# Causal attention on Trainium2: one GpSimd instruction for the P remainders of two key tiles, and another order of the row tiles for the maxima

## The chip, the cores and the metric

The kernel runs on one core of one Trainium2 chip, in one launch. The metric is device time in microseconds (us) from the start of the program to its end, as the median of several runs. Lower is better.

## What is computed

A post-norm decoder layer on x of shape (4, 1024, 512): self attention with 16 heads of 32 columns, then attention over a context with a mask, then a quantised gated feed-forward network, each with a residual sum and a layer norm. The change touches only the self attention, of which the reference says:

```python
bias = alibi_bidirectional_bias(H, S, x.dtype)
scores = jnp.einsum('bhqd,bhkd->bhqk', q, k) * (1.0 / np.sqrt(hd)) + bias[None]
attn = jax.nn.softmax(scores, axis=-1)
out = jnp.einsum('bhqk,bhkd->bhqd', attn, v)
```

The bias is causal in half of the heads (a query sees the keys up to itself) and anti-causal in the other half (a query sees the keys from itself on), with -1e9 elsewhere. So of the 8 x 8 blocks of 128 queries by 128 keys of a head only 36 are worked on.

## The kernel before

The phases run one after the other: preparation, self attention, output projection, cross attention, feed-forward. Self attention and cross attention share one function, `attention_phase`, with `causal` true or false.

There are 4 x 16 = 64 heads, taken one after the other, even ones causal and odd ones anti-causal. A head goes through two streams of 8 units each, with unit number u = 8 x head + k:

- **Maxima.** TensorE computes the scores of one row tile of 128 queries against the keys that it sees (L871, 1 to 8 blocks wide) into one of two PSUM tiles `sc`. VectorE adds the ALiBi strip and takes the row maximum (L1076). It then counts up `taken`, and TensorE may write that PSUM tile again. `rows_of` gives the order of the row tiles. When the 8 maxima of a head are there, TensorE turns them into a row (L879), ScalarE copies it (`mrow`, L987) and a DMA puts it under the queries as one more contraction row.
- **Keys.** TensorE computes the transposed scores of one key tile, less the maximum, in chunks of up to 512 queries into one of two PSUM tiles `st` (`key_scores`, L905 and the diagonal mask L908). ScalarE takes the exponential into `p32` (L979, one instruction a chunk). The upper 16 bits of each fp32 number are P's high part. GpSimd subtracts them from the number and writes the remainder to `plo` as fp16 (`low`, L1164). TensorE multiplies both parts by the values (`values`, L934 and L935) into `ob`, which holds the head's output over its 8 key tiles. `keys_of` gives the order: widths 8, 1, 7, 2, 6, 3, 5, 4 blocks. That order isn't changed.

At the end of a head ScalarE copies the high half of the output (`oraw`, L1029), VectorE adds the low half (`osum`, L1099), and with these reads TensorE may start the values of the next head. Later VectorE takes the reciprocal of the denominators (L1105) and scales the output, reading `osum` and `rden` from SBUF and writing `ost` (L1112). This last instruction stands behind the maximum of the step t with t % 8 = 2 (`SCALE`).

Each engine has one in-order queue, written out step by step. In step t TensorE issues the row scores of unit t + 19 (`SLEAD`), the key scores of unit t + 6 (`ELEAD`) and the values of unit t. VectorE does the maximum of unit t + 19, ScalarE the exponentials of unit t + 6, GpSimd the remainder of unit t + 5. For the 8 steps of a head the widths in blocks are, before the change:

```
step t % 8            0  1  2  3  4  5  6  7
row scores, maxima    2  6  3  5  4  8  1  7
key scores, exp       5  4  8  1  7  2  6  3
values                8  1  7  2  6  3  5  4
```

Below, R8 is the row scores of 8 blocks, M8 their maximum, K4 and E4 the key scores and exponentials of the key tile of 4 blocks, V8 the values of the tile of 8. `p32` and `plo` are rings of NPP buffers, each with two units in it (`spot`). Exponentials of unit u wait until the values of unit u - PAIR x NPP are done. Two lines set who waits for whom at the row scores and at the values:

```python
pe.wait_ge(taken, i * (HB * UH) + slot + 1)
pe.wait_ge(o_read, (i * HB + n) * 2 + 2)
```

The first, with `taken` started at 2, holds the row scores of a unit until the maximum of the unit two before is done. The second holds V8, the first values of a head, until both `osum` additions of the head before are done.

Of the kernel before, what the change touches and what calls it, by code (L numbers as in the profile page):

```python
# [27 lines left out]
P = 128  # L28
B, S, D = 4, 1024, 512
# [20 lines left out]
class Kit:  # L50
# [11 lines left out]
    def sb(self, name, shape, dt):  # L62
        return self.ctx.enter_context(self.nc.sbuf_tensor(name, shape, dt))
# [473 lines left out]
UH = ST  # L537
INPUT = tuple(range(ST))
BIG_FIRST = (7, 0, 6, 1, 5, 2, 4, 3), (0, 7, 1, 6, 2, 5, 3, 4)
SCALE = 2  # L540
HB = 4
NI = B * H // HB
# [2 lines left out]
PAIR = 2  # L545


def attention_phase(nc, c, name, causal, q_dram, k_dram, v_dram, out_dram, mb_dram=None, nm_dram=None, place_dram=None, kept=None, spare=None):
# [12 lines left out]

    with ExitStack() as ctx:
        kit = Kit(nc, ctx)
        SLEAD, ELEAD, NPP = 19, 6, 4
        NPR = PAIR * NPP
        PW = PAIR * S
        sem = lambda n: kit.sem(f"{name}_{n}")
        sb = lambda n, s, d: kit.sb(f"{name}_{n}", s, d)
        qa = [sb(f"qa{j}", [P, S], F16) for j in range(NQK)]
# [2 lines left out]
        vh = [sb(f"vh{j}", [P, ST, VW], F16) for j in range(NQK)]  # L572
        p32 = [sb(f"p32_{j}", [P, PW], F32) for j in range(NPP)]
        plo = [sb(f"plo{j}", [P, PW], F16) for j in range(NPP)]
        junk = [sb(f"junk{j}", [P, S], BF16) for j in range(2)]
# [49 lines left out]
        def query_range(n, kt):  # L625
            if not causal:
                return 0, S
            return (kt * P, S) if n % 2 == 0 else (0, (kt + 1) * P)

        def rows_of(u):  # L630

            n, k = divmod(u, UH)
            return n, k, (BIG_FIRST[n % 2] if causal else INPUT)[k]

        def keys_of(u):

            n, k = divmod(u, UH)
            return n, k, (BIG_FIRST[1 - n % 2] if causal else INPUT)[k]

# [33 lines left out]
        def to_finish(i, t, late):  # L673

            n, k = divmod(t, UH)
            return n - 1 if k == late and (n > 0 or not isinstance(i, int) or i > 0) else None

        def on_vector(u):

            return not causal and u % UH == 4  # L680

        def width(u):

            n, k, kt = keys_of(u)
            a, z = query_range(n, kt)
            return z - a

        def spot(u):

            return u // PAIR % NPP, 0 if u % PAIR == 0 else S  # L690

        def high_of(u):

            j, b = spot(u)
            return p32[j][:, b:b + width(u)].bitcast(BF16).rearrange("p (q h) -> p q h", h=2)[:, :, 1]

        def lows_of(u):

            j, b = spot(u)
            if on_vector(u) or not causal and u % PAIR == 0 and not on_vector(u + 1):  # L700
                return None
            if not causal and u % PAIR == 1 and not on_vector(u - 1):
                return j, 0, b + width(u)
            return j, b, b + width(u)

        def lows_by(u, vector):

            if vector:
                return sum(on_vector(m) for m in range(u + 1))
            return sum(lows_of(m) is not None for m in range(u + 1)) + (lows_of(u) is None)  # L710

        LV, LG = lows_by(HB * UH - 1, True), sum(lows_of(m) is not None for m in range(HB * UH))

        def within(last, u):
# [3 lines left out]
        with nc.Block() as block:  # L718

            @block.sync  # L720
            def _(sp):
# [28 lines left out]
                def store(i):  # L750

                    sp.wait_ge(o_scaled, i * HB + HB + 1)
                    columns = ds(i % (H // HB) * (HB * HD), HB * HD)
                    if causal:
                        out = out_dram[ds(i // (H // HB) * S, S), columns].rearrange("(t p) n -> p t n", p=P)
                    else:
                        out = kept[:, ds(i // (H // HB) * ST, ST), columns]
                    sp.dma_start(out, ost[:]).then_inc(o_out, 16)
# [7 lines left out]
                def step(i, t, last, next_batch=None, first=False):  # L766
                    n, k = divmod(t, UH)
                    if t == SCALE + 2 and not first:
                        store(i - 1)
# [85 lines left out]
            def _(pe):  # L855
                def scores(i, u):

                    n, at, qt = rows_of(u)
                    j, slot = n % NQK, u
                    if at == 0:  # L860
                        pe.wait_ge(qk_in[j], (i + n // NQK + 1) * QKS)
                    pe.wait_ge(taken, i * (HB * UH) + slot + 1)
                    if not causal:
                        nc.tensor.matmul(sc[slot % 2][:, 0:GT], qa[j][0:HD, qt * P:(qt + 1) * P], ka[j][0:HD, 0:GT], start=True, stop=True)  # L864
                        nc.tensor.matmul(sc[slot % 2][:, GT:S], qa[j][HD:2 * HD, qt * P:(qt + 1) * P], kx[j][HD:2 * HD, :],  # L865
                                         start=True, stop=True).then_inc(scored, 1)
                        return
                    k0, k1 = key_range(n, qt)
                    for k in range(k0, k1, GT):
                        w = min(GT, k1 - k)  # L870
                        mm = nc.tensor.matmul(sc[slot % 2][:, k - k0:k - k0 + w], qa[j][0:3 * HD, qt * P:(qt + 1) * P],  # L871
                                              ka[j][0:3 * HD, k:k + w], start=True, stop=True)
                    mm.then_inc(scored, 1)
# [165 lines left out]
            def _(dve):  # L1039
# [43 lines left out]
                def low(i, u):  # L1083
                    n, at, kt = keys_of(u)
                    if not on_vector(u):
                        return
                    dve.wait_ge(expd, i * CS + chunks_by(u) + 2)
                    j, b = spot(u)
                    q = slice(b, b + width(u))
                    nc.vector.tensor_tensor(plo[j][:, q], p32[j][:, q], high_of(u), ALU.subtract).then_inc(lo_v, 1)  # L1090
# [28 lines left out]
                def step(i, t, last):  # L1119
# [4 lines left out]
                    if within(last, t + ELEAD - 3):  # L1124
                        low(i, t + ELEAD - 3)
                    n = to_finish(i, t, SCALE if causal else 0)
                    if n is not None:
# [8 lines left out]
            def _(pool):  # L1136
# [21 lines left out]
                def low(i, u):  # L1158
                    if lows_of(u) is None:
                        return  # L1160
                    pool.wait_ge(expd, i * CS + chunks_by(u) + 2)
                    j, a, z = lows_of(u)
                    high = p32[j][:, a:z].bitcast(BF16).rearrange("p (q h) -> p q h", h=2)[:, :, 1]
                    nc.gpsimd.tensor_tensor(plo[j][:, a:z], p32[j][:, a:z], high, ALU.subtract).then_inc(lo_g, 1)  # L1164
# [942 lines left out]
def decoder_layer(nc, x, context, mask, Wq, bq, Wk, bk, Wv, bv, Wf, bf, w_gate, w_up, w_down, out):  # L2107
    x = x.rearrange("b s d -> (b s) d")
    context = context.rearrange("b s d -> (b s) d")
    mask = mask.rearrange("b o q k -> (b o q) k")  # L2110
    out = out.rearrange("b s d -> (b s) d")

    def scratch(name, shape, dt):
        return nc.dram_tensor(name, shape, dt).ap()

    qk_dram = [scratch(f"scr_{n}", [B, D, S], F16) for n in ("q_hi", "q_lo", "k_hi", "k_lo")]
    q2_dram = [scratch(f"scr_q2_{n}", [B, D, S], F16) for n in ("hi", "lo")]
    k2_dram = [scratch(f"scr_k2_{n}", [B, D, S], F16) for n in ("hi", "lo")]
    v_dram, v2_dram = scratch("scr_v", [B * H, P, ST, VW], F16), scratch("scr_v2", [B * H, P, ST, VW], F16)
    mb_dram, nm_dram = scratch("scr_mb", [T, S], BF16), scratch("scr_nm", [B, S, S], F16)  # L2120
    w_dram = [scratch(f"scr_w_{n}", [3 * FT, P, KT * P], F16) for n in ("hi", "lo")]
    place_dram = scratch("scr_place", [H, S], F16)
    attn, x1_dram = (scratch(n, [T, D], F32) for n in ("scr_attn", "scr_x1"))

    with ExitStack() as ctx:
        c = make_identities(nc, Kit(nc, ctx))
        preparation_phase(nc, c, x, Wq, bq, Wk, bk, Wv, bv, qk_dram, v_dram, context, k2_dram, v2_dram,
                          mask, mb_dram, nm_dram, (w_gate, w_up, w_down), w_dram)
        attention_phase(nc, c, "self", True, qk_dram[0:2], qk_dram[2:4], v_dram, attn, place_dram=place_dram)
        projection_phase(nc, c, attn, x, Wf, bf, x1_dram, q2_dram)  # L2130
        rows = Kit(nc, ctx).sb("rows", [P, RES * T], F32)
        attention_phase(nc, c, "cross", False, q2_dram, k2_dram, v2_dram, None, mb_dram, nm_dram,
                        kept=rows[:, 0:T // P * D].rearrange("p (t n) -> p t n", n=D), spare=rows[:, T // P * D:])
        feed_forward(nc, c, rows, x1_dram, w_dram, scratch, out)
# [21 lines left out]
```

## Time and profile before

| what | value |
|---|---|
| median of 3 runs | 3118.3 us (3116.58 to 3133.7) |
| the profiled execution, its own time | 3118.51 us |
| its span, first to last instruction | 3116.7 us |
| granted TensorE clock, mean | 0.935 |
| self attention, first exponential to last value matmul | 414.4 to 994.4 us |

The profiled execution lies 0.2 us above the median. Its span leaves out 1.8 us around the program. The self attention is 580 us of it, 19%. A row of the profile names line, engine, operation, output and input, and gives busy time and idle time. An engine's instructions in a row can overlap by some 40 ns in these records, since the next is fetched while one ends.

### The profile page before, as it was taken

The numbers are of one execution on the slowest core, as the hardware profiler recorded it, in microseconds if no ns is written. First come the engines' busy times: TensorE is split into PE (matmuls) and PEld (weight loads), VectorE is DVE, ScalarE is ACT, GpSimd is POOL, SyncE is SP. The second block draws the span as 40 slices with busy tenths as digits, with TensorE's granted clock in tenths as the row PEclk, the third lists the DMA queues.
The fourth block names the chain that finished last, engine by engine and source line by source line (L and its number), as shares of the span: only waits on it lengthen the run. The fifth ranks groups of instructions, "written<-read, shape, count | busy, mean of one in ns | idle before, by whom it ended". The sixth has DMA issues, their size and how long they took to land. (4 is left out here: it accounts for less than half of the span.)

```text
span 3116.7 us, 77411 instructions
## 1 busy us (share of the span) xinstructions
PE 2617.6 (84%) x24119; PEld 1411.1 (45%) x24119; DVE 2262.3 (73%) x4461; ACT 1865.0 (60%) x3767; POOL 1817.6 (58%) x1232
## 2 busy tenths in 40 slices
PE   7999578888886868999999999980999899703999
PEld 3555235555554434555555555540444344301444
DVE  8888667777775767788888888857433467697776
ACT  3444257777775435777777777764233577696333
POOL 3444479999997316999999999986100244300000
PEclk9999779999998988999999999995999999856999
DMA  8999824444445652122122232125544588797332
GB/s 303 337 335 339 271 97 135 132 128 134 128 137 163 242 199 69 53 82 69 52 85 61 56 97 55 44 59 183 206 162 161 194 271 288 252 415 279 112 124 81
DMA packets 324185, 513.52 MB, mean 165 GB/s; under 512 B 36757, under 2 KB 158485, under 8 KB 324074
## 3 DMA queue, kind: packets, MB, share of 16 engines
q1 hardware_dynamic: 320938, 505.88, 48.6%
q0 software_dynamic: 1952, 6.29, 0.6%
q8 instruction: 52, 0.85, 0.1%
q14 instruction: 59, 0.48, 0.0%
q10 hardware_dynamic: 1184, 0.01, 0.0%
HBM read 273.18 MB, written 194.28 MB: 150 GB/s over the span
## 5 line engine op out<-in xcount | busy, mean ns | idle before, releaser
L1164 POOL TENSOR_TENSOR cross_plo<-cross_p 128x2048 f16<-128x2048 f32 (+1 forms) x256 | 850.5, 3352 | 120.2 <-ACT cross_p L979 120.2
L1076 DVE CUSTOM_DVE_ANT_0 cross_junk<-cross_sc,rows 128x1024 bf16<-128x1024 f32 x512 | 622.7, 1223 | 159.2 <-PE cross_sc L865 149.7
L979 ACT ACTIVATE cross_p<-cross_st 128x512 f32<-128x512 f32 x1024 | 556.2, 595 | 205.4 <-PE cross_st L910 205.4
L1164 POOL TENSOR_TENSOR self_plo<-self_p 128x1024 f16<-128x1024 f32 (+7 forms) x512 | 577.3, 1166 | 18.7 <-ACT self_p L979 18.6
L979 ACT ACTIVATE self_p<-self_st,self_strip 128x512 f32<-128x512 f32 (+3 forms) x768 | 415.2, 582 | 148.0 <-PE self_st L908 117.2
L1076 DVE CUSTOM_DVE_ANT_0 self_junk<-self_sc,self_strip 128x1024 bf16<-128x1024 f32 (+7 forms) x512 | 371.1, 752 | 140.3 <-PE self_sc L871 135.3
L905 PE MATMUL cross_st<-cross_qa,cross_ka 97*128 97x512 f16 x1024 | 395.4, 386 | 2.4 <-ACT cross_p L979 1.9
L910 PE MATMUL cross_st<-rows,idbig 128*128 128x512 f16 x1024 | 391.0, 382 | 0.0
L934 PEld LDWEIGHTS cross_o<-cross_vh,cross_p 128*128 128x128 bf16 x4096 | 270.0, 97 | 76.3 <-issue 21.9
L934 PE MATMUL cross_o<-cross_vh,cross_p 128*128 128x65 f16 x4096 | 297.4, 191 | 5.1 <-POOL cross_plo L1164 4.7
L1774 POOL TENSOR_SCALAR v_w<-v_w 128x512 f32<-128x512 f32 x96 | 60.1, 626 | 401.5 <-ACT v_w L1751 401.4
L935 PE MATMUL cross_o<-cross_vh,cross_plo 128*128 128x33 f16 x4096 | 291.0, 179 | 0.0
L905 PE MATMUL self_st<-self_qa,self_ka 98*128 98x512 f16 (+3 forms) x768 | 243.8, 333 | 48.6 <-ACT self_p L979 44.1
L935 PEld LDWEIGHTS cross_o<-cross_vh,cross_plo 128*128 128x128 f16 x4096 | 249.2, 96 | 53.4
L871 PE MATMUL self_sc<-self_ka,self_qa 96*128 96x512 f16 (+3 forms) x768 | 212.4, 334 | 58.0 <-DVE self_strips L1050 32.0
L934 PE MATMUL self_o<-self_vh,self_p 128*128 128x65 f16 x2304 | 199.2, 192 | 39.8 <-DVE self_osum L1099 21.0
L130 PE MATMUL gt_acc<-rows,wg_hi 128*128 128x512 f16 x768 | 229.8, 381 | 1.5 <-DVE rows L124 1.5
L864 PE MATMUL cross_sc<-cross_ka,cross_qa 32*128 32x512 f16 x512 | 200.7, 393 | 28.9 <-DMA cross_kx<-scr_k_hi 18.5
L865 PE MATMUL cross_sc<-cross_kx,cross_qa 32*128 32x512 f16 x512 | 200.6, 393 | 0.0
L934 PEld LDWEIGHTS self_o<-self_vh,self_p 128*128 128x128 bf16 x2304 | 163.1, 97 | 74.1 <-issue 43.8
L935 PE MATMUL self_o<-self_vh,self_plo 128*128 128x33 f16 x2304 | 191.9, 179 | 0.0
L905 PEld LDWEIGHTS cross_st<-cross_qa,cross_ka 97*128 97x128 f16 x1024 | 99.7, 97 | 190.1 <-ACT cross_p L979 95.4
(256 smaller groups left out, 5843.8 us busy)
## 6 DMA issues: line engine op xcount, KB each, us to landing
self_strip<-self_strips SPq DMA_DIRECT2D x68, 516.0 KB, 3.2
scr_gate<-gt_y SPq DMA_DIRECT2D x96, 256.0 KB, 2.1
v_w<-scr_gate SPq DMA_DIRECT2D x96, 256.0 KB, 4.1
scr_h<-v_w SPq DMA_DIRECT2D x96, 256.0 KB, 4.2
j_h<-scr_h SPq DMA_DIRECT2D x48, 512.0 KB, 9.5
d_o<-scr_o SPq DMA_DIRECT2D x9, 1536.0 KB
scr_up<-v_y SPq DMA_DIRECT2D x48, 256.0 KB, 4.3
j_u<-scr_up SPq DMA_DIRECT2D x24, 512.0 KB, 12.1
```

The source lines that it names most:

```text
L130: mm = nc.tensor.matmul(out, a, b, start=(n == 0), stop=(n == len(terms) - 1))
L864: nc.tensor.matmul(sc[slot % 2][:, 0:GT], qa[j][0:HD, qt * P:(qt + 1) * P], ka[j][0:HD, 0:GT], start=True, stop=True)
L865: nc.tensor.matmul(sc[slot % 2][:, GT:S], qa[j][HD:2 * HD, qt * P:(qt + 1) * P], kx[j][HD:2 * HD, :], start=True, stop=True).then_inc(scor ...
L871: mm = nc.tensor.matmul(sc[slot % 2][:, k - k0:k - k0 + w], qa[j][0:3 * HD, qt * P:(qt + 1) * P], ka[j][0:3 * HD, k:k + w], start=True, st ...
L905: mm = nc.tensor.matmul(out[:, 0:w], lhs, qa[j][0:KR, q0:q1], start=True, stop=causal)
L910: mm = nc.tensor.matmul(out[:, 0:w], c["idbig"][:], nm[kt][:, q0:q1], start=False, stop=True)
L934: nc.tensor.matmul(out[:, qt % 4, :], high[:, q], vh[n % NQK][:, kt, :], start=first, stop=False, skip_group_check=True)
L935: mm = nc.tensor.matmul(out[:, qt % 4, 0:HD + 1], rest[:, q], vh[n % NQK][:, kt, 0:HD + 1], start=False, stop=last_kt, skip_group_check=True)
L979: nc.scalar.activation(p32[j][:, b + q0 - a:b + q1 - a], stp[cc % 2][:, 0:q1 - q0], ACT.Exp, bias=bias, scale=SM).then_inc(expd, 1)
L1076: nc.vector.tensor_tensor_reduce(junk[slot % 2][:, 0:w], sc[slot % 2][:, 0:w], bias, 1.0, -3e38, ALU.add, ALU.max, qmax[n % 2][:, qt:qt + ...
L1164: nc.gpsimd.tensor_tensor(plo[j][:, a:z], p32[j][:, a:z], high, ALU.subtract).then_inc(lo_g, 1)
L1774: nc.gpsimd.tensor_scalar(wk[n % NW][:], wk[n % NW][:], 65536.0, MAGIC, ALU.mult, ALU.add).then_inc(inc, 1)
```

## The change

In the causal phase the ring gets 8 buffers in place of 4, each 1152 columns wide (9 blocks) in place of 2048. The second unit of a pair stands right behind the first. GpSimd no longer runs a remainder for each unit: at the even unit it does nothing, and at the odd one it does both in one instruction over 1152 columns, since each pair of key tiles has 9 blocks (8 + 1, 7 + 2, 6 + 3, 5 + 4). The values of an even unit therefore wait for the remainder of the pair. The cross attention did this already, and nothing changes there. The row tiles for the maxima come in another order, with widths 8, 7, 1, 2, 6, 5, 3, 4.

```diff
 BIG_FIRST = (7, 0, 6, 1, 5, 2, 4, 3), (0, 7, 1, 6, 2, 5, 3, 4)
+BIG_TWICE = (7, 6, 0, 1, 5, 4, 2, 3), (0, 1, 7, 6, 2, 3, 5, 4)
...
-        SLEAD, ELEAD, NPP = 19, 6, 4
+        SLEAD, ELEAD, NPP = (19, 6, 8) if causal else (19, 6, 4)
         NPR = PAIR * NPP
-        PW = PAIR * S
+        PW = S + P if causal else PAIR * S
...
-            return n, k, (BIG_FIRST[n % 2] if causal else INPUT)[k]
+            return n, k, (BIG_TWICE[n % 2] if causal else INPUT)[k]
...
-            return u // PAIR % NPP, 0 if u % PAIR == 0 else S
+            return u // PAIR % NPP, 0 if u % PAIR == 0 else (width(u - 1) if causal else S)
...
-            if on_vector(u) or not causal and u % PAIR == 0 and not on_vector(u + 1):
+            if on_vector(u) or u % PAIR == 0 and not on_vector(u + 1):
                 return None
-            if not causal and u % PAIR == 1 and not on_vector(u - 1):
+            if u % PAIR == 1 and not on_vector(u - 1):
                 return j, 0, b + width(u)
```

The widths by step are, after it:

```
step t % 8            0  1  2  3  4  5  6  7
row scores, maxima    2  6  5  3  4  8  7  1
key scores, exp       5  4  8  1  7  2  6  3
values                8  1  7  2  6  3  5  4
```

GpSimd's queue in the first four heads, one head of it, before (`self_plo` is the remainder, `self_p32` the numbers; the number behind the name is the buffer):

```order
L1164 TENSOR_TENSOR self_plo0<-self_p32_0 128x1024
L1164 TENSOR_TENSOR self_plo0<-self_p32_0 128x128
L1164 TENSOR_TENSOR self_plo1<-self_p32_1 128x896
L1164 TENSOR_TENSOR self_plo1<-self_p32_1 128x256
L1164 TENSOR_TENSOR self_plo2<-self_p32_2 128x768
```

and after:

```order
L1165 TENSOR_TENSOR self_plo5<-self_p32_5 128x1152
L1165 TENSOR_TENSOR self_plo6<-self_p32_6 128x1152
L1165 TENSOR_TENSOR self_plo7<-self_p32_7 128x1152
L1165 TENSOR_TENSOR self_plo0<-self_p32_0 128x1152
L1165 TENSOR_TENSOR self_plo1<-self_p32_1 128x1152
```

Eight instructions of 128 to 1024 columns for a head have become four of 1152.

VectorE's queue around the scaling of a head's output (`self_junk`, `self_qmax` are the maxima, `self_sc` the row scores), before:

```order
L1076 ISA self_junk0,self_qmax0<-self_sc0,self_strip0 128x768
L1076 ISA self_qmax0 128x1
L1076 ISA self_junk1,self_qmax0<-self_sc1,self_strip0 128x384
L1076 ISA self_qmax0 128x1
L1105 RECIPROCAL self_rden1<-self_oraw1 128x8
L1112 TENSOR_TENSOR self_ost<-self_osum1,self_rden1 128x8x32
L1076 ISA self_junk0,self_qmax0<-self_sc0,self_strip0 128x640
L1076 ISA self_qmax0 128x1
L1076 ISA self_junk1,self_qmax0<-self_sc1,self_strip0 128x512
```

and after:

```order
L1077 ISA self_junk0,self_qmax1<-self_sc0,self_strip1 128x768
L1077 ISA self_qmax1 128x1
L1077 ISA self_junk1,self_qmax1<-self_sc1,self_strip1 128x640
L1077 ISA self_qmax1 128x1
L1106 RECIPROCAL self_rden0<-self_oraw0 128x8
L1113 TENSOR_TENSOR self_ost<-self_osum0,self_rden0 128x8x32
L1077 ISA self_junk0,self_qmax1<-self_sc0,self_strip1 128x384
L1077 ISA self_qmax1 128x1
L1077 ISA self_junk1,self_qmax1<-self_sc1,self_strip1 128x512
```

The maxima of 3 and 5 blocks have changed sides of the scaling.

TensorE's queue around the turn of the maxima (L879, after it L880), between V3 and V5, before:

```order
L935 MATMUL self_o<-self_vh,self_plo 128x33
L871 MATMUL self_sc<-self_ka,self_qa 128x128
L879 MATMUL self_st<-idf,self_qmax 8x128
L905 MATMUL self_st<-self_qa,self_ka 128x256
L908 MATMUL self_st<-self_tri,idbig 128x128
```

and after:

```order
L936 MATMUL self_o<-self_vh,self_plo 128x33
L872 MATMUL self_sc<-self_ka,self_qa 128x512
L872 MATMUL self_sc<-self_ka,self_qa 128x384
L880 MATMUL self_st<-idf,self_qmax 8x128
L906 MATMUL self_st<-self_qa,self_ka 128x256
L909 MATMUL self_st<-self_tri,idbig 128x128
```

The row scores of 7 blocks now stand ahead of the turn, one step after those of 8, and those of 1 block follow V5.

## Rows read from the trace of the kernel before

**Rows 1.** The page: slices of GpSimd, 40 over the span, in tenths

```profile
POOL 3444479999997316999999999986100244300000
```

**Rows 2.** Busy time of the engines in a stretch of the self attention

```profile
600.00:700.00 100.00, 84.02 (x1164) 52.97 (x1164) 75.99 (x222) 76.20 (x167) 99.98 (x89) 1.00 0.43 132
```

**Rows 3.** Groups by form, 500 to 900 us: count, busy us, mean ns, idle before

```profile
L979 ACT ACTIVATE self_p<-self_st,self_strip 128x512 f32<-128x512 f32 x266 | 175.4, 688 | 59.4 <-PE self_st L908 48.0 <-PE self_st L905 11.4
...
L1164 POOL TENSOR_TENSOR self_plo<-self_p 128x1024 f16<-128x1024 f32 x44 | 90.6, 2059 | 0.1
...
L1164 POOL TENSOR_TENSOR self_plo<-self_p 128x512 f16<-128x512 f32 x44 | 45.8, 1041 | 0.0
...
L1112 DVE TENSOR_TENSOR self_ost<-self_osum,self_rden 128x256 f32<-128x256 f32 x44 | 30.9, 703 | 6.4 <-DVE self_rden L1105 2.4
```

**Rows 4.** Timeline of GpSimd, self attention: start us, us, instruction, count

```profile
425.46 1.90 POOL L1164 TENSOR_TENSOR self_plo<-self_p 128x1024 f16<-128x1024 f32 x1 [0.45 <-ACT self_p L979]
...
613.76 3.07 POOL L1164 TENSOR_TENSOR self_plo<-self_p 128x512 f16<-128x512 f32 x2
```

**Rows 5.** Timeline of VectorE, one head

```profile
613.59 0.55 DVE L1076 CUSTOM_DVE_ANT_0 self_junk<-self_sc,self_strip 128x384 bf16<-128x384 f32 x1
...
614.07 0.20 DVE L1105 RECIPROCAL self_rden<-self_oraw 128x8 f32<-128x8 f32 x1
614.48 0.60 DVE L1112 TENSOR_TENSOR self_ost<-self_osum,self_rden 128x256 f32<-128x256 f32 x1 [0.21 <-DVE self_rden L1105]
615.00 0.81 DVE L1076 CUSTOM_DVE_ANT_0 self_junk<-self_sc,self_strip 128x640 bf16<-128x640 f32 x1
...
616.86 1.23 DVE L1076 CUSTOM_DVE_ANT_0 self_junk<-self_sc,self_strip 128x1024 bf16<-128x1024 f32 x1 [0.43 <-PE self_sc L871]
...
618.92 1.09 DVE L1076 CUSTOM_DVE_ANT_0 self_junk<-self_sc,self_strip 128x896 bf16<-128x896 f32 x1 [0.61 <-PE self_sc L871]
...
619.94 0.48 DVE L1099 TENSOR_TENSOR self_osum<-self_o,self_oraw 128x128 f32<-128x128 f32 x2
```

**Rows 6.** Timeline of TensorE, the same head

```profile
611.53 0.20 PE L934 MATMUL self_o<-self_vh,self_p 128*128 128x65 f16 x1 [0.67 <-ACT self_p L979]
...
615.88 0.61 PE L871 MATMUL self_sc<-self_ka,self_qa 96*128 96x512 f16 x2
...
617.62 0.19 PE L934 MATMUL self_o<-self_vh,self_p 128*128 128x65 f16 x1
...
618.15 0.55 PE L871 MATMUL self_sc<-self_ka,self_qa 96*128 96x512 f16 x2
618.54 0.33 PE L905 MATMUL self_st<-self_qa,self_ka 98*128 98x384 f16 x1
...
620.55 0.20 PE L934 MATMUL self_o<-self_vh,self_p 128*128 128x65 f16 x1 [0.56 <-DVE self_osum L1099]
```

**Rows 7.** Timeline of ScalarE, the same head

```profile
612.80 2.31 ACT L979 ACTIVATE self_p<-self_st,self_strip 128x512 f32<-128x512 f32 x4 [1.09 <-PE self_st L908]
...
617.06 0.25 ACT L987 ACTIVATE self_mrow<-self_st 8x128 f16<-8x128 f32 x1
...
618.97 0.58 ACT L979 ACTIVATE self_p<-self_st,self_strip 128x384 f32<-128x384 f32 x1 [0.32 <-PE self_st L908]
619.45 0.43 ACT L1029 COPY self_oraw<-self_o 128x132 f32<-128x132 f32 x2
```

**Rows 8.** Timeline: GpSimd and VectorE subtractions and scalings side by side

```profile
980.28 1.47 POOL L1164 TENSOR_TENSOR self_plo<-self_p 128x768 f16<-128x768 f32 x1
...
980.83 1.19 DVE L1112 TENSOR_TENSOR self_ost<-self_osum,self_rden 128x256 f32<-128x256 f32 x1
...
995.62 0.42 DVE L1112 TENSOR_TENSOR self_ost<-self_osum,self_rden 128x256 f32<-128x256 f32 x1
...
2082.21 3.60 POOL L1164 TENSOR_TENSOR cross_plo<-cross_p 128x2048 f16<-128x2048 f32 x1
...
2083.41 3.48 DVE L1090 TENSOR_TENSOR cross_plo<-cross_p 128x1024 f16<-128x1024 f32 x1
```

## Prediction

> **What bounds the kernel now.** I read the page's slices first: GpSimd is full in the slices of the self attention and full again in the cross attention [rows 1]. The change touches only the first, which is 580 us of 3117. Then the engines by stretch there: GpSimd is busy 99.98 of 100 us, TensorE 84, VectorE and ScalarE 76 [rows 2]. A head takes 620.55 - 611.53 = 9.02 us, from its V8 to the next [rows 6], and GpSimd's eight remainders fill all of it.
>
> A full engine doesn't show yet who waits for it, so I walked one head in the timelines of the four engines. All times that follow are from the start of V8 at 611.53. TensorE never waits for a remainder there: the waits named at V8 are for ScalarE or for VectorE's `osum` [rows 6]. GpSimd acts on the others in another way, through L1112, the scaling of a head's output. It starts at 2.95 us while the remainder of 512 columns runs. That one began at 613.76 and takes 1.04, so it ends at 614.80 [rows 3, 4]. L1112 ends at 615.08, 0.28 after it, and takes 0.60 here and 703 ns in the mean, but 0.42 where GpSimd is done [rows 3, 5, 8]. Then M5 runs, from 3.47 to 4.28, and R8 starts at 4.35, when M5 has freed its PSUM tile [rows 5, 6]. From R8 on the chain is M8, R7 (it waits for M8, which ends at 618.09; R7 starts at 618.15), K3, E3, `oraw`, `osum`, V8 [rows 5 to 7]. So the head's time is the way from V8 to R8, 4.35 us, and the way from R8 to V8, 4.67 us.
>
> **L1112 waits for a whole GpSimd instruction.** The trace shows it three times with other lengths. At 980.83 L1112 meets a remainder of 768 columns that runs from 980.28 to 981.75, takes 1.19 us and ends at 982.02, 0.27 after it [rows 8]. At 2083.41 a VectorE subtraction of 1024 columns with both inputs in SBUF meets a remainder of 2048 that ends at 2085.81. It takes 3.48 us and ends at 2086.89, again behind it [rows 8]. The remainder of 1024 columns, which comes next after L1112's wait, takes 2059 ns in the mean, but 1.90 where no L1112 runs [rows 3, 4]: GpSimd then waits a little for VectorE.
>
> The Trainium skill ("SBUF — State Buffer", section "Who interferes with whom") says that a VectorE instruction with two SBUF inputs and a GpSimd instruction that reads SBUF exclude each other for a whole instruction. By that rule longer GpSimd instructions are longer waits for L1112, and the trace agrees in the 1.19 us above. Were the port only shared out in parts, L1112 would be late by some tenths and the second rival below would hold.
>
> **The change part by part.**
>
> *Pairs, GpSimd's own time.* 1024 columns cost 1.90 us alone and 2048 cost 3.60 [rows 4, 8], so 1.66 ns a column and 1.90 + 128 x 1.66 ns = 2.11 us for 1152. The row with the disturbed 1024 columns would give 2059 + 213 = 2.27, the two ends of this cost. I take 2.11. Records overlap by 40 ns, so a head's four cost 8.3 us, or 8.45 with one wait for L1112, in place of 9.02. That is 0.6 to 0.75 us a head, but only if GpSimd's sum is what sets the head.
>
> *Pairs, L1112.* The pair of the tiles of 5 and 4 blocks is ready when E4 ends. E4 is the first of the four exponentials at 612.80 and takes 0.69, so it ends at 1.96 [rows 3, 7]. GpSimd is free by then: the pair before (6 + 3) is ready when E3 ends, 1.0 us before V8 (619.55 against 620.55) [rows 6, 7], so it runs to about 1.2 us after V8, 0.8 ahead of E4's end. With the 0.1 us from an exponential to its remainder the pair runs from 2.05 to 4.16. L1112 now stands behind M5, not M3, and is ready 0.26 later (0.81 for 0.55 us), at 3.21 [rows 5]. It falls into the middle of the pair, waits for its end, and ends at 4.16 + 0.27 = 4.43. Before it ended at 3.55. Queued behind it on VectorE are M3 and M4, and for M3 waits R8 on TensorE.
>
> *Order of the maxima, V8 to R8.* M3 starts 0.08 before L1112's recorded end, at 4.35, takes 0.55 and ends at 4.90. R8 starts 0.07 later, at 4.97. That is 0.62 later than now. TensorE has nothing that it may do in the meantime, since V6, the last item before R8, is through by then.
>
> *Order of the maxima, R8 to V8.* Now R7 waits for M8, and K3 follows R7 after 0.39 us (618.15 to 618.54) [rows 6]. After the change R7 is one step earlier, M7 follows M8 at once, and only the short R1 waits for M8. That would save some 0.33 on K3. Against it R7 now stands ahead of the turn of the maxima. Turn and `mrow` (617.06, 0.25 us) come 0.33 later, and with them the second chunk of K6, V5 (6.09 now) and the second exponential of E6 [rows 6, 7]. K3 then starts 0.21 earlier and E3, held by E6, 0.19 earlier. `osum` loses no wait worth naming: it starts at 619.94, 0.06 after `oraw` ends at 619.88, so M7 ahead of it hardly held it [rows 5, 7]. The way from R8 to V8 becomes 4.67 - 0.19 = 4.48 us.
>
> *The ring of 8.* Exponentials may run 16 units ahead of the values in place of 8, but key scores stand only 6 ahead in TensorE's queue. It is worth nothing: the cover is that ELEAD sets the distance. The wait of an even unit's values for the pair costs nothing either. The pair 5 + 4 ends at 4.16 and V5 reads it after 6 us.
>
> *Ends of the phase.* In the last head no maxima run. GpSimd is then the last but one, and one pair of 2.11 us in place of a backlog saves about 1 us.
>
> **Sum.** A head takes 4.97 + 4.48 = 9.45 us in place of 9.02, 0.43 more. L1112 and R8 meet in heads 1 to 60, so 60 x 0.43 = 26 us, less 1 us at the end: 25 us. Against the profiled execution's own 3118.5 that gives 3143.5 us. The median of the runs is 0.2 below it, so I say 3143.
>
> **Rivals.**
>
> *1. L1112's wait stays short: faster.* If L1112 waits no longer than alone (0.42 to 0.49 us), it ends at 3.70, M3 at 4.17 and R8 starts at 4.24, 0.11 earlier than now. With the 0.19 above this is 0.30 a head, 60 x 0.30 + 1 = 19 us: 3099 us. The place is L1112 and the price is the wait for the pair. It decides at 4.0 us: if L1112 ends before that (the pair must have begun by 1.6, before E4's end at 1.96), the 0.43 is gone. For it speaks that the chain through R7 really becomes shorter. Against it speak the 1.19 and 3.48 us [rows 8].
>
> *2. GpSimd's sum sets the head: much faster.* It is busy 99.98% now [rows 2]. At 8.45 us a head or 8.3, the 62 middle heads save 35 to 45 us: some 3078 us. Against it speaks that the walk from V8 to V8 has no wait for a remainder in it, only VectorE's for the port.
>
> *3. No change that can be told.* The two parts cancel if the pair starts earlier or L1112's place moves, so that L1112 loses only some 0.2 to 0.5 us of the 0.88: 3103 to 3133 us. For this GpSimd would have to be in another phase than at E4's end, for instance still in the pair 6 + 3 when L1112 comes, ending between 3.1 and 3.8. With four pairs that take 8.45 us and a head of over 9 it has idle time there, which speaks against it.
>
> **How the numbers follow.** A measurement of this kernel tells about 0.5% (15.6 us) from no change. My forecast, slower by the wait of L1112, gets 0.70, with its own range 3131 to 3160: the pair's upper price (0.16 us more) and 0.1 us a head of error in the walk behind R8 make 0.26 x 60 = 16 us above, and 0.2 us a head of error in the walk 12 us below. Rival 3 gets 0.12, rival 1 0.13 and rival 2 0.05. Slower by over 0.5% (above 3134) takes 0.68, the rest of the forecast and rival 3 make 0.15 within 0.5%, and 0.17 is left for faster. The range that leaves out rival 2, most of rival 1 and a little above is 3101 to 3160.
>
> **What the profile after would show.** Right: remainders of 1152 columns at 2.1 us, four a head; GpSimd busy some 90% in the self attention, with idle time ahead of the pair 5 + 4; L1112 at a mean of 1.2 us (3.21 to 4.43) in place of 703 ns; a new wait of R8 for a maximum (L872 for L1077) of 0.6 us a head; the way from R8 to V8 0.2 us shorter; the self attention about 605 us long, and everything behind it unchanged. Wrong: L1112 at 0.5 to 0.8 us would fell the forecast for rival 1. GpSimd still at 99% with a head of 8.4 us would be rival 2. A remainder of 1152 columns far from 2.1 us would shift everything, as would a lower granted clock than 1.00 in the middle of the phase [rows 2], since TensorE is idle for longer each head.

## The result and the profile after

The changed kernel takes 3145.05 us in the median of 8 runs (3140.61 to 3156.56), against 3117.7 us (3115.68 to 3133.7, 8 runs) before: a ratio of 1.0083, 95% interval 1.0065 to 1.0101. It is slower by 0.8%. Its profiled execution took 3142.04 us, with a span of 3140.3.

First the slices of GpSimd from the page, for [rows 1], and the busy times in one stretch of the self attention, for [rows 2]. The busy times stand in the order TensorE, its weight loads, VectorE, ScalarE, GpSimd; behind them come the granted clock, the DMA share and GB/s. GpSimd is no longer full, and the granted TensorE clock is 1.00 as before.

```profile
POOL 3444479988988324999999999995200144400000
```

```profile
600.00:700.00 100.00, 81.90 (x1110) 50.50 (x1109) 80.00 (x211) 72.79 (x159) 90.28 (x43) 1.00 0.42 129
```

The groups by form from 500 to 900 us, for [rows 3]: mean ns behind the busy time.

```profile
L1165 POOL TENSOR_TENSOR self_plo<-self_p 128x1152 f16<-128x1152 f32 x170 | 362.4, 2151 | 39.9 <-ACT self_p L980 37.5
...
L1113 DVE TENSOR_TENSOR self_ost<-self_osum,self_rden 128x256 f32<-128x256 f32 x42 | 53.5, 1274 | 6.2 <-DVE self_rden L1106 2.4
```

L1113, the scaling that was L1112, went from 703 to 1274 ns. The waits of the same 400 us show who pays. Behind the names stand the total in us, the number of waits and the longest:

```profile
PE self_sc L872 <- DVE self_qmax L1077: 29.8, 53, 0.7
...
DVE self_osum L1100 <- ACT self_oraw L1030: 19.5, 42, 0.7
```

Neither of these two waits is in the list of the same stretch before. The first is R8 waiting for M3 in 42 of its 53 cases, 0.67 us each; the other 11 are R2, with 0.16. Now one head, and the turn to the next, in the timelines. VectorE, for [rows 5]:

```profile
610.42 0.20 DVE L1106 RECIPROCAL self_rden<-self_oraw 128x8 f32<-128x8 f32 x1
610.74 1.30 DVE L1113 TENSOR_TENSOR self_ost<-self_osum,self_rden 128x256 f32<-128x256 f32 x1
611.97 0.54 DVE L1077 CUSTOM_DVE_ANT_0 self_junk<-self_sc,self_strip 128x384 bf16<-128x384 f32 x1
...
614.71 1.09 DVE L1077 CUSTOM_DVE_ANT_0 self_junk<-self_sc,self_strip 128x896 bf16<-128x896 f32 x1
615.72 0.28 DVE L1077 CUSTOM_DVE_ANT_0 self_junk<-self_sc,self_strip 128x128 bf16<-128x128 f32 x1
616.66 0.49 DVE L1100 TENSOR_TENSOR self_osum<-self_o,self_oraw 128x128 f32<-128x128 f32 x2 [0.65 <-ACT self_oraw L1030]
```

TensorE, for [rows 6]: V8, R8, R7, the turn, K3, V8, and in the next head R8, K3, V8.

```profile
607.63 0.20 PE L935 MATMUL self_o<-self_vh,self_p 128*128 128x65 f16 x1 [0.46 <-DVE self_osum L1100]
...
612.57 0.60 PE L872 MATMUL self_sc<-self_ka,self_qa 96*128 96x512 f16 x2 [0.65 <-DVE self_qmax L1077]
613.36 0.54 PE L872 MATMUL self_sc<-self_ka,self_qa 96*128 96x512 f16 x2
613.73 0.27 PE L880 MATMUL self_st<-idf,self_qmax 128*8 128x128 f32 x1
...
615.45 0.34 PE L906 MATMUL self_st<-self_qa,self_ka 98*128 98x384 f16 x1 [0.34 <-ACT self_p L980]
...
617.28 0.20 PE L935 MATMUL self_o<-self_vh,self_p 128*128 128x65 f16 x1 [0.47 <-DVE self_osum L1100]
...
622.23 0.61 PE L872 MATMUL self_sc<-self_ka,self_qa 96*128 96x512 f16 x2 [0.71 <-DVE self_qmax L1077]
...
624.75 0.34 PE L906 MATMUL self_st<-self_qa,self_ka 98*128 98x384 f16 x1
...
626.57 0.20 PE L935 MATMUL self_o<-self_vh,self_p 128*128 128x65 f16 x1 [0.37 <-DVE self_osum L1100]
```

GpSimd, for [rows 4], and ScalarE, for [rows 7]:

```profile
609.65 6.42 POOL L1165 TENSOR_TENSOR self_plo<-self_p 128x1152 f16<-128x1152 f32 x3 [0.74 <-ACT self_p L980]
```

```profile
608.89 2.26 ACT L980 ACTIVATE self_p<-self_st,self_strip 128x512 f32<-128x512 f32 x4 [0.97 <-PE self_st L909]
...
616.37 0.43 ACT L1030 COPY self_oraw<-self_o 128x132 f32<-128x132 f32 x2
```

These rows show the following. GpSimd idles for 0.74 us until E4 has ended and then starts the pair 5 + 4, at 609.65 or 2.02 us after V8. That pair takes 2.11 us, so it ends at 611.76. L1113 starts at 610.74 into the middle of it and ends at 612.04, 0.28 us behind it. M3 follows at 611.97, and R8, after 0.65 us of waiting, at 612.57: 4.94 us after V8, where it was 4.35. The two heads take 9.65 and 9.29 us.

The heads repeat in a cycle of four, from V8 to V8 (the engines' loops run over four heads). In the middle of the phase the four took 9.00, 9.02, 8.88 and 9.19 us before, 9.02 in the mean, and take 9.64, 9.30, 9.50 and 9.39 us after, 9.46 in the mean. The way from V8 to R8 went from 4.38 to 4.95 us and the way from R8 to V8 from 4.65 to 4.51. Below, "a head of so many us" is the mean of such a cycle at full clock. The self attention, from its first exponential to its last value matmul, is 610 us long, where it was 580.

### The profile page after: what moved, and what is told of

It reads as the page before. It is cut to its first block and busy times, and to the rows that moved or that the text cites. A ratio compares the mean times of both kernels' runs of the same rounds, so it can differ in the third digit from the quotient of the medians.

```text
span 3140.3 us, 76959 instructions
## 1 busy us (share of the span) xinstructions
PE 2638.8 (84%) x24119; PEld 1414.9 (45%) x24119; DVE 2301.1 (73%) x4461; ACT 1867.6 (59%) x3767; POOL 1785.2 (57%) x976
## 5 line engine op out<-in xcount | busy, mean ns | idle before, releaser
L1165 POOL TENSOR_TENSOR self_plo<-self_p 128x1152 f16<-128x1152 f32 x256 | 545.3, 2149 | 76.4 <-ACT self_p L980 72.8
L980 ACT ACTIVATE self_p<-self_st,self_strip 128x512 f32<-128x512 f32 (+3 forms) x768 | 411.7, 582 | 160.4 <-PE self_st L909 125.6
L906 PE MATMUL self_st<-self_qa,self_ka 98*128 98x512 f16 (+3 forms) x768 | 255.2, 339 | 34.4 <-ACT self_p L980 24.7
```

What stands on the lines that cost most here:

```text
L906: mm = nc.tensor.matmul(out[:, 0:w], lhs, qa[j][0:KR, q0:q1], start=True, stop=causal)
L980: nc.scalar.activation(p32[j][:, b + q0 - a:b + q1 - a], stp[cc % 2][:, 0:q1 - q0], ACT.Exp, bias=bias, scale=SM).then_inc(expd, 1)
```

## The experiments

Most runs edit the changed kernel; the three that edit the kernel before say so. Times are medians, and the ratio is to the kernel before, run in the same job, with its 95% interval. Three dots in an edit stand for lines that are left out.

**The two parts of the change, one at a time.** With the pairs and the old order:

```diff
-            return n, k, (BIG_TWICE[n % 2] if causal else INPUT)[k]
+            return n, k, (BIG_FIRST[n % 2] if causal else INPUT)[k]
```

> The pairs and the ring of 8, with the row tiles in the old order (8, 1, 7, 2, 6, 3, 5, 4). Wait theory (L1113 waits for the whole pair 5 + 4): L1113 is ready at 2.95 us after V8 behind M3, ends with the pair at 4.43, and M5 (0.81 us) instead of M3 (0.55) stands between it and R8, so R8 starts at 5.2; the way from R8 to V8 stays 4.67. A head of 9.9 us, 3165 to 3175 us. Rival (the pairs gain and the new order of the maxima is what costs): no slower than 3118 us.

Measured: 3177.39 us, ratio 1.0171 (1.0121 to 1.0221). L1113 in this kernel, by form from 500 to 900 us:

```profile
L1113 DVE TENSOR_TENSOR self_ost<-self_osum,self_rden 128x256 f32<-128x256 f32 x41 | 63.2, 1541 | 6.0 <-DVE self_rden L1106 2.2
```

The pairs alone cost twice what the whole change costs, a little more than expected, with a head of 9.88 us. L1113 comes 0.27 us earlier and meets the same pair, hence 1541 in place of 1274 ns, and M5 behind it is longer than M3. The rival, in which the order is what costs, falls.

The new order alone, in the kernel before:

> The kernel before with only the row tiles in the new order, one remainder a unit. Wait theory: L1112 is ready at about 3.2 us, just as the remainder of 512 columns ends, so it hardly waits; the others' chain would be some 8.7 us, and GpSimd's own sum of 8.85 to 9.02 us a head then sets the pace: 3107 to 3118 us, GpSimd still 99% busy. Rival (the order costs): over 3130 us.

Measured: 3118.56 us, ratio 0.9987 (0.9967 to 1.0006), which can't be told from no change. GpSimd is busy 100.00 of 100 us there, from 600 to 700 us. The time is 0.6 us above my range, and one step was wrong: the scaling was to wait hardly at all, and it takes 850 ns in the mean. Although the order alone should leave the other engines a shorter head, the head stays at 9.02 us. GpSimd's sum is the likely hold; how it acts is shown below, with the scaling of the kernel before in step 0.

**L1113 taken away.** The changed kernel without the scaling:

```diff
...
-                    nc.vector.tensor_tensor(ost[:, :, m * HD:(m + 1) * HD], osum[n % 2][:],
-                                            rden[n % 2][:].unsqueeze(2).to_broadcast([P, ST, HD]), ALU.mult).then_inc(o_scaled, 1)
+                    dve.sem_inc(o_scaled, 1)
```

> The changed kernel without L1113: the scaling of the output is left out (ost is zeroed once, and the self attention's output is 0), all other work stays. Wait theory: nothing of VectorE's waits for GpSimd any more, R8 starts at about 4.2 us, R8 to V8 takes 4.5: a head of 8.7 us, 3095 to 3100 us. Rival (the 0.4 us a head come from elsewhere, such as the pair's lateness or the turn behind R7): 3135 us or more.

Measured: 3098.6 us, ratio 0.9926 (0.9906 to 0.9946). Leaving out one VectorE instruction of 0.42 us a head turns 0.8% slower into 0.7% faster. The difference to the changed kernel is 46 us over 60 heads, 0.77 us a head (by the cycles of four heads 9.46 against 8.65, 0.80), more than the instruction's own time. So most of it lies in what that instruction waits for.

The same in the kernel before, and in the pairs with the old order. The fourth combination, the new order alone without the scaling, was not run:

> The kernel before without L1112: the scaling is left out (ost is zeroed once, the self attention's output is 0). GpSimd's eight remainders then never wait for VectorE and sum to 8.86 us in place of 9.02: 3106 to 3111 us, GpSimd 99.9% busy. With the changed kernel without scaling at 3098.6 us, this says how much the pairs and the order give together where the port isn't contended: 8 to 12 us. Rival (before the change the port cost nothing): 3118 us.

> The changed kernel with the row tiles in the old order and without L1113 (the scaling is left out, ost is zeroed once, the self attention's output is 0). Wait theory: without the port's wait R8 starts at 4.2, but R8 to V8 stays at 4.6 to 4.67 through R7's wait for M8: 8.80 to 8.87 us a head, 3105 to 3112 us, where the new order gave 3098.6. Rival (the order is worth nothing and the pairs gain alone once the port is free): 3096 to 3102 us.

Measured: 3110.57 us, ratio 0.9973 (0.9963 to 0.9983), and 3109.58 us, ratio 0.9971 (0.9959 to 0.9982). Both times are as expected. The stretch 600 to 700 us of the first has GpSimd full also without L1112:

```profile
600.00:700.00 100.00, 83.61 (x1180) 52.90 (x1181) 70.66 (x216) 77.00 (x171) 99.89 (x92) 1.00 0.44 136
```

In the second GpSimd is at 94% and the head is no shorter: 8.88 us, against 8.86 in the first. So GpSimd, though full in the first, isn't shown to be its bound. The remainder of 8 blocks starts there 0.09 to 0.13 us after its exponential has ended, so GpSimd has caught up once a head. And in the second, where GpSimd has idle time, the chain of the other engines still takes 8.88 us. The two happen to need about the same time. With both parts of the change the head is 8.65 us. So where nothing of VectorE's waits for GpSimd, the pairs alone bring nothing that can be told, and with the order they bring 10 us (by the spans of the profiled executions, 3108.7 and 3108.3 against 3098.3) to 14 us (by the ratios). What the order would bring without the pairs isn't shown; as an estimate, GpSimd's eight remainders, which filled the 8.86 us, would have held the head there.

**L1113 moved.** To step 0, behind M2:

```diff
-                    n = to_finish(i, t, SCALE if causal else 0)
+                    n = to_finish(i, t, 0 if causal else 0)
```

> The changed kernel with L1113 in step 0, behind M2, in place of step 2, behind M5. Wait theory: it is ready at 0.3 us after V8, meets the pair 6 + 3, which ends at 1.2 to 1.6, and ends at 1.5 to 1.9; M6 starts late by 0.3 to 0.7, which the gap before R8 takes up. A head of 8.7 us, 3097 to 3105 us, with L1113 still at 1.1 us or more in the mean. Rival (the wait costs the same wherever it stands): 3143 us.

Measured: 3115.21 us, ratio 0.9969 (0.9947 to 0.9991); its profiled execution took 3111.16. L1113 takes about as long as in the changed kernel (1239 ns in the mean), and the 0.8% are gone: the same wait costs far less where R8 doesn't stand right behind it. The rival falls. But I had expected 10 us less, and a head of 8.7 us where it is 8.96. The list of waits has what I left out:

```profile
PEld self_sc L872 <- DVE self_qmax L1077: 19.0, 78, 0.3
```

Of these 78 waits, 45 are R4's, one a head and 0.27 us each: a late M6 makes M5 late, and R4 waits for M5's tile ahead of K7, V6 and R8. In the changed kernel R4 has no such wait. 22 are R2's, which the changed kernel has too, and 11 are R3's, for M6. R8 starts 4.46 us after V8, against 4.15 without the scaling. I had put only M3 ahead of R8.

To step 1, behind M6 (the same line with 1):

> The changed kernel with L1113 in step 1, behind M6, in place of step 2. Wait theory: it is ready at about 2.4 us after V8, 0.4 after the pair 5 + 4 began, and ends with it at 4.4; now M5 and M3 both stand behind it, and R4, which needs M5's tile, waits too and holds K7 and V6. R8 starts at 5.7 to 6.3 in place of 4.97, a head takes 10.1 to 10.7 us: 3185 to 3220 us. Rival (an earlier place gives the wait more room and costs no more): 3145 us or less.

Measured: 3293.38 us, ratio 1.0561 (1.0544 to 1.0579). The direction is as the theory says, the size isn't: 150 us more than the changed kernel, not 40 to 75. Two heads show why, in busy time by stretch from V8 to V8 (the third number from the right is the granted clock, as a share of 2.4 GHz):

```profile
594.07:606.27 12.20, 9.26 (x105) 5.70 (x106) 8.65 (x21) 6.91 (x17) 8.66 (x5) 0.86 0.28 82
606.27:617.16 10.89, 7.59 (x105) 4.63 (x106) 8.29 (x21) 6.89 (x16) 8.47 (x5) 1.00 0.46 145
```

TensorE does the same 105 matmuls in both. Where its clock stayed at 2.4 GHz the head takes 10.9 us, 0.2 above my upper end. In the other one the granted clock is 0.86 in the mean, so part of it ran at 1.2 GHz, and it takes 12.2. In the steady part of the phase only one head in six is at full clock; the others take 11.7 to 13.0 us. The timeline of TensorE has the idle stretch in the head at full clock: R4 starts after 1.99 us of waiting for M5.

```profile
611.48 0.39 PE L872 MATMUL self_sc<-self_ka,self_qa 96*128 96x512 f16 x1 [1.99 <-DVE self_qmax L1077]
```

In the changed kernel TensorE idles for at most 0.7 us at a time from 500 to 900 us, and the clock is at 0.98 to 1.00 in each 100 us. With the pairs in the old order it is 0.9 us at most, TensorE is busy 76.75 of 100 us, and the clock is 1.00. That the long idle stretch is what lowers the clock is the likely reading. No run here varies its length alone.

To step 3, behind M3, with the reciprocal left in step 2. The scaling moves into a function of its own, `scale_late`; this is where it is called:

```diff
...
+                    n = to_finish(i, t, SCALE + 1) if causal else None
+                    if n is not None:
+                        scale_late(i, n)
```

> The changed kernel with the reciprocal left in step 2 and L1113 in step 3, behind M3. Wait theory: L1113 is ready at 4.0 to 4.1 us, just ahead of the end of the pair 5 + 4 at 4.13, ends at 4.4, and only M4 stands behind it; R8 starts at 4.2 to 4.3: a head of 8.75 us, 3097 to 3106 us, L1113 at 0.4 to 0.6 us. If it comes behind 4.13 instead, it meets the pair 8 + 1, ends at 6.5 and holds M4 and M8: over 3170 us. Rival (the wait isn't what costs): 3143 us.

Measured: 3106.61 us, ratio 0.9963 (0.9943 to 0.9984). The full computation is faster than the kernel before. L1113 took 740 ns in the mean, more than I said: it was ready at 3.67 us after V8 and not at 4.0, as the reciprocal no longer stands right ahead of it, and it lost some 0.3 us to the pair's end. R8 starts at 4.11, as early as without the scaling. But M4, which stood behind L1113, holds R7: the way from R8 to V8 is 4.71 us in place of 4.51. The head takes 8.83 us.

**The pair that L1113 meets, split.** This is the sharpest test: L1113 keeps its place, three of the four pairs stay, and only the pair 5 + 4 is two remainders again.

```diff
             j, b = spot(u)
+            if causal and u % UH >= UH - 2:
+                return j, b, b + width(u)
```

> The changed kernel with the pair of the tiles of 5 and 4 blocks split again into two remainders (640 and 512 columns); the other three pairs and L1113's place stay. Wait theory: at 3.1 us after V8 L1113 meets only the remainder of 512 columns, which ends at about 3.4, and ends at 3.6; R8 starts at 4.2, GpSimd's sum is some 8.6 us: a head of 8.7 us, 3097 to 3105 us, L1113 at 0.5 to 0.6 us. Rival (the pairs or the order cost in another way, such as the even units' values being late): 3135 us or more.

Measured: 3104.05 us, ratio 0.9954 (0.9940 to 0.9967), the lowest median of the kernels with the full computation, though the interval of the one with the scaling in step 3 overlaps it. The time is in my range; the head of 8.89 us and R8 at 4.37 are 0.2 above what I expected. By form from 500 to 900 us:

```profile
L1167 POOL TENSOR_TENSOR self_plo<-self_p 128x1152 f16<-128x1152 f32 x135 | 288.2, 2148 | 13.5 <-ACT self_p L982 9.8
...
L1167 POOL TENSOR_TENSOR self_plo<-self_p 128x640 f16<-128x640 f32 x46 | 57.7, 1254 | 0.0
L1167 POOL TENSOR_TENSOR self_plo<-self_p 128x512 f16<-128x512 f32 x45 | 46.9, 1041 | 0.1
L1115 DVE TENSOR_TENSOR self_ost<-self_osum,self_rden 128x256 f32<-128x256 f32 x45 | 31.3, 695 | 6.6 <-DVE self_rden L1108 2.6
```

L1113 (here L1115) is back at 695 ns. The rival, by which the pairs cost through the late values of the even units, falls. The traces agree: in the steady part of every kernel here TensorE starts the values of a tile 1.8 us or more after their remainder has ended, 2.4 us or more in the changed kernel.

**The ring, and L1112's place before the change.** The ring with 4 buffers of 1152 columns in place of 8:

> The changed kernel with 4 buffers of 1152 columns in place of 8. The key scores stand 6 units ahead in TensorE's queue, so that the exponentials never reach the ring's end with 8 units either: 3140 to 3147 us, as the changed kernel. Rival (the longer ring gives something that the port's wait hides): 3150 us or more.

Measured: 3147.4 us, ratio 1.0104 (1.0080 to 1.0129). The interval holds the changed kernel's 1.0083, and L1113 is at 1273 ns as there: the ring's length has no effect that these runs can tell.

The kernel before with L1112 in step 0:

> The kernel before with L1112 in step 0, behind M2, in place of step 2. GpSimd's sum sets the pace there, so that the place of L1112 matters little: it meets a short remainder and costs GpSimd some 0.1 to 0.2 us a head as before: 3108 to 3120 us, GpSimd over 99% busy. Rival (the place of L1112 before M5 costs before the change too): under 3105 us.

Measured: 3116.62 us, ratio 0.9994 (0.9984 to 1.0003), so the time doesn't move. L1112 by form from 500 to 900 us:

```profile
L1112 DVE TENSOR_TENSOR self_ost<-self_osum,self_rden 128x256 f32<-128x256 f32 x44 | 56.3, 1279 | 7.7 <-DVE self_rden L1105 3.6
```

It takes 1279 ns there, as long as in the changed kernel, while I had it meet a short remainder. This trace also shows how a full GpSimd holds the head. Here are four heads early in the phase and four later ones, in busy time by engine, and below them the busy time of the four scalings in each:

```profile
512.68:548.10 35.42, 29.77 (x420) 18.87 (x421) 27.68 (x81) 27.49 (x61) 35.42 (x33) 1.00 0.42 135
601.79:637.89 36.10, 30.31 (x421) 19.09 (x421) 30.31 (x81) 27.50 (x61) 36.10 (x33) 1.00 0.41 132
```

```profile
512.68:548.10 35.42, 2.66 (x4) 1.00 0.42 135
601.79:637.89 36.10, 5.52 (x4) 1.00 0.41 132
```

The early heads take 8.86 us, as without the scaling at all, and GpSimd can't keep up with them: the lead that a tile's remainder has over its values falls from 3.65 us at 512.68 to 2.46 at 601.79. In the same time L1112 grows from 0.67 to 1.38 us, and from then on a head takes 9.03 us, GpSimd's sum. The lead stays at 2.3 to 2.5 us, so TensorE waits for no remainder. What the late GpSimd holds is L1112, and through it VectorE's queue. That is my reading of this trace; no run holds L1112's wait fixed and varies the rest. A list of waits must be read with care here: at V8 this run's list names GpSimd for the weight load (at 610.78), although V8's own remainder had ended at 608.36 and the matmul itself waited for ScalarE or `osum`, as in the kernel before.

## Why the prediction was right, and where its steps were not

The forecast was 3143 us and a head of 9.45 us. Measured were 3145.05 us and 9.46. The mechanism was right, and part of the agreement is luck: two terms were off by some 0.05 us a head in opposite directions, the effect at the end of the phase had the wrong sign, and one at its start was not in the sum.

*The pair's price* (2.11 us for 1152 columns): 2.11 where nothing disturbs it, and 2151 ns in the mean with the one pair a head that waits for VectorE. Right.

*L1113 meets the pair 5 + 4* (pair from 2.05 to 4.16, L1113 from 3.21 to 4.43): in the head shown the pair runs from 2.02 to 4.13 and L1113 from 3.11 to 4.41. Right, and shown as a cause by splitting just that pair and by taking L1113 away.

*R8 at 4.97 in place of 4.35*: 4.94 and 4.95 in the two heads. Right. Over the cycle of four heads R8 was at 4.38 before and is at 4.95, so it moved by 0.57 us, not 0.62: the head that I had walked has an earlier R8 than the mean.

*From R8 to V8, 4.48 in place of 4.67*: 4.51 in place of 4.65 over the cycle, a gain of 0.14 and not 0.19. The end value was nearly right, and its steps were not. I had said that K3 starts 0.21 earlier and that M7 hardly held `osum`. K3 stands 2.88 us after R8 in the first head and 2.52 in the second, 2.66 over the cycle of four, against 2.63 before. So the later turn took back all that the shorter R1 gave. In my walk I had used one head only, and the neighbouring kind takes the two chunks of K6 in the other order, which makes K3 wait for the longer exponential (the 0.34 us at 615.45). What became shorter is the end: `osum` now starts 0.29 after `oraw` starts (616.37 to 616.66), where it was 0.49 (619.45 to 619.94) [rows 5, 7]. `osum` is two additions, each for one half of `oraw`. Before the change the first could have started when the first half was copied, but M7 ran until 620.01, so the start at 619.94 was M7's doing. I had read it as the end of `oraw`, 0.06 us earlier. The list of waits agrees: `osum` waits for `oraw` in all 42 heads after, and M1 is long through by then. From K3 to V8 it is 1.85 us in place of 2.02 over the cycle. That the order gains is shown by the pairs without scaling: the medians are 3109.58 us in the old order and 3098.6 in the new, and a head takes 8.88 and 8.65 us. Of these 0.23 us, 0.15 lie behind R8. That they come through `osum` and not K3 is read from the traces and was not tried alone.

*The ring costs and gives nothing*: shown within the interval.

*Ends of the phase, 1 us saved*: not borne out. The last two heads take 8.82 and 9.44 us where they took 8.38 and 8.29, the last one with a granted clock of 0.68. At the other end the first exponential comes at 409.9 us in place of 414.4. It is early in the trace of the order alone too (411.7) and isn't in that of the pairs in the old order (415.8), so it seems to belong to the order; why is open. These effects partly cancel.

*Rival 1* (3099 us if L1113 hardly waits) gave the right time for the case that it described: 3098.6 with L1113 away. The real kernels that came near it, with the split pair and with step 3, stay 5 to 8 us above, since L1113 waits 0.3 us in them too, and holds R8 in the first and R7 in the second.

*Rival 2*, GpSimd's sum as the bound, was wrong for the changed kernel, where GpSimd is at 90%. But I had given it too little weight for the kernel before: with the order alone and with L1112 in step 0 the head stays at GpSimd's 9.02 us. My argument, that no wait for a remainder is in the walk, doesn't exclude it, since a late GpSimd can hold the others through L1112. Nor is GpSimd's sum a bound that the pairs could have turned into a gain by themselves. Without the scaling the head is 8.86 us with eight remainders and 8.88 with four pairs: the 0.16 us below 9.02 come from taking L1112 away, and none of the 0.6 us of GpSimd time that the pairs save shows up until the order is changed too.

*Rival 3* has an error in its range. By the terms of the forecast a loss of 0.5 us at L1112 gives some 3121 us, not 3133.

The Trainium skill ("SBUF — State Buffer", section "Who interferes with whom") says that a VectorE instruction with two SBUF inputs and a reading GpSimd instruction exclude each other for a whole instruction. The 1274 and 1541 ns of L1113 here agree.

## What to carry to other kernels

Merging instructions on a full engine saves their fixed cost, but it also lengthens what another engine may have to wait for in one piece: look up every VectorE instruction with two SBUF inputs, what stands behind it in its queue, and which GpSimd instruction runs when it comes. Where the gain is lost that way, move the waiting instruction to where nothing urgent stands behind it, or keep just the one long instruction that it meets short. And when an engine is full, ask what the next chain takes before counting the saving: here, with the scaling left out, the pairs took 0.6 us a head off GpSimd and the head stayed at 8.86 to 8.88 us until the order was changed too. Last, walk as many heads as the program's loop has: here a single head was off the mean by up to 0.17 us.

## What the runs showed of the hardware that was not expected

VectorE's instruction gets its turn between two GpSimd instructions that stand back to back. In the changed kernel the exponentials of the pair 8 + 1 end 0.6 us before that pair starts, so it is ready before L1113 ends, and L1113 still goes first: it ends 0.28 us behind the pair 5 + 4, and the pair 8 + 1 takes 2.29 us where an undisturbed one takes 2.11. The 0.28 us are the same whatever the length of the GpSimd instruction that it met (512, 768 and 1152 columns). So in the steady part it never waited for two in a row.

With L1113 in step 1, and idle stretches of TensorE of 2.0 us, the granted clock fell to 0.86 from 500 to 900 us, while it stayed at 1.00 where the longest idle stretch was 0.9 us (the pairs in the old order). The head went from 10.9 to 12.2 us by that, about as much as the 1.4 us that the wait itself had added (9.46 to 10.9).
